# Routing logits of a linear-attention layer: from tokens on the output partitions to gate weights held in the array

## The reference

```
x = x + _layernorm(_L1_attn_ref(_layernorm(x), ...))          # linear attention, here "the linear layer"
xf = _layernorm(x).reshape(n, 256)                            # n = 8192 tokens
probs = softmax(xf @ Wg)                                      # Wg is 256 x 8: the routing logits
topv, topi = top_k(probs, 2)
... every token's row is sent to its two experts, positions by a running count ...
```

## Time and profile before

| | |
|---|---|
| median of 3 runs | 4360.51 us (4354.82 to 4367.13) |
| profiled execution | span 4370.4 us (no time other than the span is given for this execution) |
| PE busy | 91% of the span |
| DVE, ACT, POOL busy | 63%, 49%, 27% |
| mean granted TensorE clock | 0.957 of full speed |
| logits matmuls (L1585) | 256 records, first at 1622.4 us, last at 3465.3 us |

### The profile page before, as it was taken

How to read it: one execution, slowest core, us unless ns; L and a number is a source line. 1 busy time by engine, 2 the same in 40 slices (tenths; PEclk the granted TensorE clock), 3 DMA queues, 4 the chain that set the end, 5 groups by cost and what they waited for, 6 DMA issues and landing times. The chain is left out here.

```text
span 4370.4 us, 72366 instructions
## 1 busy us (share of the span) xinstructions
PE 3998.7 (91%) x27380; PEld 3076.0 (70%) x27380; DVE 2755.4 (63%) x8052; ACT 2120.4 (49%) x4002; POOL 1188.2 (27%) x1104
## 2 busy tenths in 40 slices
PE   5999999999995699999999999999999599999992
PEld 2344444444443588888888888888888599999992
DVE  4788888788781655556565555556665465555555
ACT  1566666666663445445454544445454133333333
POOL 3233343343422411111111111111111123333334
PEclk8899999999996899999999999999999799999996
DMA  4443443353230200000000000000000133333336
GB/s 76 87 94 64 84 103 61 73 115 70 42 80 24 78 11 25 21 20 25 24 21 18 18 16 21 11 19 19 19 19 31 34 74 70 63 63 73 63 66 184
DMA packets 176459, 226.91 MB, mean 52 GB/s; under 512 B 27292, under 2 KB 152571, under 8 KB 176112
## 3 DMA queue, kind: packets, MB, share of 16 engines
q1 hardware_dynamic: 148080, 185.86, 18.1%
q0 software_dynamic: 26736, 31.70, 4.7%
q10 hardware_dynamic: 1296, 4.72, 0.3%
HBM read 90.63 MB, written 87.05 MB: 41 GB/s over the span
## 5 line engine op out<-in xcount | busy, mean ns | idle before, releaser
L838 ACT ACTIVATE probs<-a_scores 128x1024 f32<-128x1024 f32 (+3 forms) x768 | 615.5, 812 | 334.6 <-PE a_scores L742 328.6
L996 DVE CUSTOM_DVE_ANT_0 a_scores<-a_scores,mask 128x384 f32<-128x384 f32 (+3 forms) x1024 | 480.5, 514 | 115.5 <-PE a_scores L728 109.8
L742 PEld LDWEIGHTS a_scores<-q_st,k_st 50*128 50x128 f32 x1536 | 147.9, 189 | 381.1 <-issue 245.0
L1732 ACT ACTIVATE l_o<-l_num,l_den 128x64 f32<-128x64 f32 x960 | 223.6, 317 | 352.2 <-DVE l_den L2124 349.6
L275 POOL TENSOR_TENSOR l_ln_rstd<-l_ln_ve,minus_half 128x4 f32<-128x4 f32 x80 | 84.1, 1051 | 1116.0 <-DVE l_ln_ve L248 1115.7
L999 DVE TENSOR_REDUCE mx<-a_scores 128x2 f32<-128x1024 f32 x256 | 310.5, 1223 | 83.1 <-PE a_scores L728 81.8
L742 PE MATMUL a_scores<-q_st,k_st 50*128 50x512 f32 (+3 forms) x1536 | 346.7, 449 | 9.2 <-DVE mx L996 4.4
L728 PE MATMUL a_scores<-k_st,q_st 48*128 48x512 f32 (+3 forms) x1536 | 304.7, 395 | 47.7 <-ACT probs L838 28.5
L762 PE MATMUL a_out<-probs,v_aug 128*32 128x512 f32 (+3 forms) x3072 | 344.8, 522 | 2.2 <-POOL probs L929 2.1
L929 POOL TENSOR_SCALAR_AFFINE_SELECT probs<-probs 128x512 f32<-128x512 f32 x256 | 163.6, 639 | 524.8 <-ACT probs L838 516.3
L2421 PE MATMUL e_out<-e_weights_hi,e_hT_hi 128*128 128x256 f32 x1088 | 303.9, 279 | 0.0
(11 more groups left out here) (268 smaller groups left out, 10506.6 us busy)
## 6 DMA issues: line engine op xcount, KB each, us to landing
q_st<-parts SPq DMA_DIRECT2D x192, 128.0 KB, 4.5
k_st<-parts SPq DMA_DIRECT2D x192, 128.0 KB, 6.2
expert_rows_scratch<-empty_row SPq DMA_DIRECT2D x34, 520.0 KB, 9.2
l_x<-x_scratch SPq DMA_DIRECT2D x32, 512.0 KB, 3.9
e_weights<-in_L_ffn_W_dram SPq DMA_DIRECT2D x16, 1024.0 KB, 6.8
e_rows<-expert_rows_scratch SPq DMA_DIRECT2D x24, 390.0 KB
e_rows<-expert_rows_scratch SPq DMA_DIRECT2D x16, 520.0 KB
x_in<-in_L_attn_x_dram SPq DMA_DIRECT2D x8, 1024.0 KB, 5.7
```

The costliest lines, as they stand in the source:

```text
L742: last = nc.tensor.matmul(psum_r[:, R.slot(u), h2, 0:w], k_st[rows, 2 * hg + pair, i * P:(i + 1) * P], q_st[rows, 2 * hg + pair, q0:q0 + w ...
L838: nc.scalar.activation(probs[:, k % 3, 2 * pair:2 * pair + 2, 0:w], psum_r[:, R.slot(u), :, 0:w], ACT.Exp).then_inc(R.evacuated[R.slot(u)], 1)
L996: last = nc.vector.tensor_tensor_reduce(s, s, mask[:, HALF - w:HALF], 1.0, LEAST, ALU.add, ALU.max, out[:, h2, :])
L1732: last = nc.scalar.activation(o[:, j % 2, head:head + DH1], psum_n[:, NUM.slot(n), h * DV:h * DV + DH1], ACT.Copy, scale=den[:, n % 2, 1, ...
```

## The change

The gate weights become the stationary operand and the tokens stream through. `wg` is padded from 8 to 32 columns (`EW = 32`, the rest filled with zeros by DVE ahead of the load), and the four token tiles of a group go to four groups of 32 columns of the array: tile j is written to partitions 32j to 32j+31 of one PSUM slot. That gives the logits with experts on the partitions and tokens on the free axis, as one unit `LT` in place of two units `L`. DVE copies the 128 x 128 block to SBUF (`lgT`, which lies in the bytes of `scores[:, 1]`, and so of `nT2`), PE turns it back by one transpose (unit `L`, `turn_logits`), and DVE copies the wanted 128 x (4 x 8) of it into `lg`. The number of units in the ring stays the same.

The place moves too: `LT` stands ahead of the last two `KT` units (now called `KE`), the transpose `L` behind them, and the wait for the last three `KT` units stays behind the transpose. `last_logits` waits for each `T3` unit by itself, just ahead of the half that reads it; in the tail this replaces the wait for both.

```diff
-    OWN = [("QK", NQK), ("KT", 8), ("O", 8), ("W", 2), ("T2", CD), ("F1", MF), ("F2", 2)]
+    OWN = [("QK", NQK), ("KT", 6), ("KE", 2), ("O", 8), ("W", 2), ("T2", CD), ("F1", MF), ("F2", 2)]
-    OF_LAST = [("T3", CD), ("L", 2)]
+    OF_LAST = [("T3", CD), ("LT", 1), ("L", 1)]
...
-        wg = sb("l_wg", [P, CD, E])
+        wg = sb("l_wg", [P, CD, EW])
...
+        lgT = scores[:, 1, 0, 0, :]
...
+                nc.vector.memset(wg[:, :, :], 0.0).then_inc(filled, 1)
...
-                    for i in range(2):
-                        u = U["L"] + i
-                        G.wait_free(pe, r, u)
-                        for jj in range(2):
-                            j = 2 * i + jj
-                            for c in range(CD):
-                                last = nc.tensor.matmul(psum_g[:, G.slot(u), jj * E:(jj + 1) * E],
-                                                        nT2[:, c, j * P:(j + 1) * P], wg[:, c, :],
-                                                        start=(c == 0), stop=(c == CD - 1))
-                        last.then_inc(G.full[G.slot(u)], 1)
+                    u = U["LT"]
+                    G.wait_free(pe, r, u)
+                    for c in range(CD):
+                        G.wait_evacuated(pe, r, U["T3"] + c)
+                        for j in range(G4):
+                            last = nc.tensor.matmul(psum_g[EW * j:EW * j + EW, G.slot(u), 0:P],
+                                                    wg[:, c, :], nT2[:, c, j * P:(j + 1) * P],
+                                                    start=(c == 0), stop=(c == CD - 1),
+                                                    skip_group_check=True)
+                    last.then_inc(G.full[G.slot(u)], 1)
+
+                def turn_logits(r, U):
+
+                    u = U["L"]
+                    G.wait_evacuated(pe, r, U["LT"])
+                    G.wait_free(pe, r, u)
+                    nc.tensor.transpose(psum_g[:, G.slot(u), 0:P], lgT[:, :], ident[:, :]
+                                        ).then_inc(G.full[G.slot(u)], 1)
...
+                    for i in range(8):
+                        u, j, half = kt_unit(U, i), i // 2, i % 2
+                        if i == 6 and not first:
+                            last_logits(g, U)
...
                     if not first:
-                        last_logits(g, U)
-
-                    for u in range(U["KT"] + 8 - R, U["KT"] + 8):
-                        G.wait_evacuated(pe, g, u)
+                        turn_logits(g, U)
+
+                    for i in range(8 - R, 8):
+                        G.wait_evacuated(pe, g, kt_unit(U, i))
...
                 turn_last(NGR - 1, NGR - 1, units_after)
-                for c in range(CD):
-                    G.wait_evacuated(pe, NGR - 1, units_after["T3"] + c)
                 last_logits(NGR - 1, units_after)
+                turn_logits(NGR - 1, units_after)
...
                 def keep_logits(r, g, U):
-                    for i in range(2):
-                        u = U["L"] + i
-                        G.wait_full(dve, r, u)
-                        nc.vector.tensor_copy(lg[:, 2 * i:2 * i + 2, :],
-                                              psum_g[:, G.slot(u), 0:2 * E].rearrange(
-                                                  "p (j e) -> p j e", j=2)).then_inc(G.evacuated[G.slot(u)], 1)
-                    G.wait_evacuated(dve, r, U["L"] + 1)
+                    u = U["LT"]
+                    G.wait_full(dve, r, u)
+                    nc.vector.tensor_copy(lgT[:, :], psum_g[:, G.slot(u), 0:P]
+                                          ).then_inc(G.evacuated[G.slot(u)], 1)
+                    u = U["L"]
+                    G.wait_full(dve, r, u)
+                    nc.vector.tensor_copy(lg[:, :, :],
+                                          psum_g[:, G.slot(u), 0:P].rearrange(
+                                              "p (j e) -> p j e", j=G4)[:, :, 0:E]
+                                          ).then_inc(G.evacuated[G.slot(u)], 1)
+                    G.wait_evacuated(dve, r, u)
```

More of the change, by code:

```diff
@@ L1169, in linear_layer @@
     NQK = 2 * NP
+    EW = 32
     LATE = 2
-    OWN = [("QK", NQK), ("KT", 8), ("O", 8), ("W", 2), ("T2", CD), ("F1", MF), ("F2", 2)]
+    OWN = [("QK", NQK), ("KT", 6), ("KE", 2), ("O", 8), ("W", 2), ("T2", CD), ("F1", MF), ("F2", 2)]
     OF_NEXT = [("T1", CD), ("V", 8 - LATE), ("VE", LATE)]
-    OF_LAST = [("T3", CD), ("L", 2)]
-    ORDER = OWN[0:1] + OF_LAST[0:1] + OWN[1:2] + OF_LAST[1:2] + OWN[2:3] + OF_NEXT[0:1] + OWN[3:4] + OF_NEXT[1:2] + OWN[4:5] + OF_NEXT[2:3] + OWN[5:]
+    OF_LAST = [("T3", CD), ("LT", 1), ("L", 1)]
+    ORDER = (OWN[0:1] + OF_LAST[0:1] + OWN[1:2] + OF_LAST[1:2] + OWN[2:3] + OF_LAST[2:3] + OWN[3:4] +
+             OF_NEXT[0:1] + OWN[4:5] + OF_NEXT[1:2] + OWN[5:6] + OF_NEXT[2:3] + OWN[6:])
     LAST_NORMS = (1, 2, 3, 5, 8, 9, 10, 12)
@@ L1329, in _ @@
                 nc.vector.tensor_copy(token[:, :], spot[:, :]).then_inc(filled, 1)
-                dve.wait_ge(filled, 2)
+                nc.vector.memset(wg[:, :, :], 0.0).then_inc(filled, 1)
+                dve.wait_ge(filled, 3)
         G = Ring(sem, "l_general", R, N_ALL)
@@ L1378, in v_unit, with kt_unit @@
             return U["V"] + i if i < 8 - LATE else U["VE"] + i - (8 - LATE)
+        def kt_unit(U, i):
+            return U["KT"] + i if i < 6 else U["KE"] + i - 6
         def of_group(view, g):
@@ L1408, in _ @@
                                          allow_slow_non_contiguous=True).then_inc(raw_loaded[0], 16)
-                for dst, w in ((raw_o[:, :, :], Wo), (raw_f[0], Wf1), (raw_f[1], Wf2), (wg[:, :, :], Wg)):
+                for dst, w in ((raw_o[:, :, :], Wo), (raw_f[0], Wf1), (raw_f[1], Wf2), (wg[:, :, 0:E], Wg)):
                     sp.dma_start(dst, w.rearrange("(c p) n -> p c n", p=P)).then_inc(load, 16)
@@ L1604, in group @@
                         G.wait_evacuated(pe, g, u)
[L1606 to L1614, removed]
+                    for i in range(8):
+                        u, j, half = kt_unit(U, i), i // 2, i % 2
+                        if i == 6 and not first:
+                            last_logits(g, U)
+                        G.wait_free(pe, g, u)
+                        for m in range(4):
+                            last = nc.tensor.transpose(psum_g[:, G.slot(u), m * P:(m + 1) * P],
+                                                       kT[:, 4 * half + m, j * P:(j + 1) * P],
+                                                       ident[:, :])
+                        last.then_inc(G.full[G.slot(u)], 1)
                     if not first:
-                        last_logits(g, U)
-                    for u in range(U["KT"] + 8 - R, U["KT"] + 8):
-                        G.wait_evacuated(pe, g, u)
+                        turn_logits(g, U)
+                    for i in range(8 - R, 8):
+                        G.wait_evacuated(pe, g, kt_unit(U, i))
                     if s == 0:
@@ L1758, in group @@
                     for i in range(8):
-                        u = U["KT"] + i
-                        j, half = i // 2, i % 2
+                        u, j, half = kt_unit(U, i), i // 2, i % 2
                         G.wait_full(act, g, u)
```

## The result

The changed kernel takes 4343.83 us (median of 20 runs, 4339.01 to 4363.79), the kernel before in the same comparison 4356.62 us (20 runs, 4348.15 to 4374.97). The ratio is 0.9977, with a 95% interval of 0.9966 to 0.9988: 0.23% or 10 us faster (5 to 15 us); the two medians by themselves are 12.8 us apart. Forecast were 7.7 us, and a change of less than 0.3% as the likely outcome; the measured gain agrees with both. Counted from its own starting point the range is 16.5 us faster to 5.5 us slower, and 10 us faster lies in it. As the experiments show, the 7.7 us were reached by a sum in which one term was too large and one was missing.

What follows compares the result with a forecast made beforehand. The prediction took PE's order to bound the kernel: 5.6 us from the groups plus 2.1 us from the tail, 7.7 us off the 4360.5 us median, gave 4352.8 us, with a range of 4344 to 4366 us.

Steps and rivals of the forecast that it cites:

- What bounds the kernel: Groups with logits: PE, busy 96%, sets the pace; an earlier `score(1)` moves all behind it.
- LT at 0.67 us: Each group: `LT`'s 16 records take PE 0.67 us, gaps included, where the old logits took 1.88; bounds 0.43 and 1.98.
- one after another: Rival, `LT`: column groups load weights serially, 1.98 us; 13.0 us slower in all, 4373.5 us; chance 0.08.
- the records stagger: Rival, `LT`: a matmul's second record waits for its first, 9 rounds, 1.2 us; no change, 4360.5 us; chance 0.10.
- no wait: Start of `LT`: its slot, `KT`'s unit 3, is copied out by 2240.20, before PE gets there at 2240.28.
- The trip to VectorE: Between `LT` and transpose `L`: DVE's copy, 0.29 us, is done 0.6 us ahead, covered by two `KE` units.
- The stall on ScalarE: Before `score(1)`: PE stands 0.7 us for ACT's last `kt` copy, leaving 0.37 us gain per group, 5.6 us in all.
- The tail: After the last group, once, at half clock: `choose` comes 2.1 us earlier; bounds 0.7 us lost and 2.5 us gained.
- At nothing: the wider `wg` and its memset.: Gate weights' load and setup: memset under 0.2 us if uncovered, DMA has the same rows; priced at nothing.
- The wait for ACT doesn't bind: Rival, before `score(1)`: ACT has `kt` out sooner, PE gains 1.09 us per group; 18.5 us, 4342 us; chance 0.04.
- The gain is taken back in the loop: Rival, chunk loop: something started ahead of the logits sets it, only the tail's gain stays; 4358 us; chance 0.12.

Runs made afterwards that it cites:

- the one-group run: Changed kernel with all four token tiles of `LT` in one group of 32 columns instead of four, only the first tile's logits as the reference's; one run, 4384.27 us.

## Why the prediction was right, and where it wasn't

*What bounds the kernel.* Right. PE's order sets the pace, and every experiment that moved `score(1)` moved the group by the same amount, to within 0.06 us.

*LT at 0.67 us.* Right, and for the reason given: four groups together. Counted as in the working, with the gap ahead, it is 0.67 us: the last transpose ahead of `LT` starts at 2228.90 and the next behind it at 2229.68, less the 0.11 us of one transpose. The 0.58 us above are without that gap. The array's part was taken as 0.43 us, and the 16 records start in four rounds of four, at 2229.10, 2229.23, 2229.34 and 2229.45. The rivals "one after another" (1.98) and "the records stagger" (1.2) are both out, and the one-group run shows what the first would have cost: 1.96 us, counted with the gap ahead. The Trainium skill's rule in "TensorE: Matmul & The Clock Gate", The mechanism, that a weight load overlaps matmuls in flight only in another row group, doesn't hold here: 16 loads of 110 ns in the same rows lie within 0.38 us, those of the second round from 2229.13 on, while the products that started at 2229.10 are in flight. The Trainium skill says in "TensorEngine Tiling (Array Packing)", Key Properties, that a change of tiling mode drains the array. The trace has 0.20 us from the last start of one form to the first of the next, on either side of `LT`, where one transpose follows another after 0.11. So it is some 0.09 us a side, where the working had 0.12 and 0.14; and the side ahead can't be told from a wait, as the trace has `LT`'s first load released by ACT's copy of its slot [0.17 <-ACT l_k L1776], where the working had "no wait".

*The trip to VectorE.* Right: 0.29 us copy, no wait.

*The stall on ScalarE.* Right as a mechanism, and ACT's last copy ended 5.21 us after `KT`'s start where the working has 5.23. The step that failed is the one from there to `score(1)`: "`score(1)` starts at 2242.71 to 2242.75", up to 0.05 us behind ACT's end. It is 0.21 us (2230.37 + 1.07 = 2231.44 to 2231.65), and 0.20 to 0.24 in every group. That made the term 5.6 us; it is 15 x 0.21 = 3.2 us. Why it takes that long isn't shown. It isn't the same at every wait: behind DVE's copy of `LT` the transpose follows 0.06 us later in all groups of the version with `LT` behind `KT`.

*The tail.* 2.1 us forecast, 6.49 - 4.45 = 2.04 measured.

*"At nothing: the wider `wg` and its memset."* Wrong. This is the term that was missing. I priced the memset and the DMA and not that the tiles behind move. It is the larger part of the gain: 0.41 us per group in the run with the wider tile alone (123.43 - 123.02), 0.35 in the changed kernel (0.56 less the 0.21 of the edited stretch), some 6 us over the groups.

The sum by the traces is 3.2 + 2.0 + 6 = 11 us, against 10 (5 to 15) measured. That the forecast's 7.7 lies inside the interval is luck in part: a 2.4 us overestimate and a 6 us omission partly cancelled. Without the side effect the change as such is worth 5 us by the traces, which this kernel's measurement can't tell from none.

*The other rivals.* "The wait for ACT doesn't bind" is out (0.77 us of idle time in each of 15 groups). "The gain is taken back in the loop" is out: `score(1)` to output projection is 45.32 us in both.

## What to carry to other kernels

Before pricing work taken off the busiest engine, look for the wait that this work covers; here half of the 1.88 us, 0.92, was cover for ScalarE's copies, and the cheapest remedy was to issue the next product that doesn't need them ahead of the wait. A cover moved to one trip uncovers another, so compare the lengths of both, hand-over included (from a copy's end to PE's next product it was 0.21 us behind ScalarE here and 0.06 behind VectorE). And when a tile changes its size, cut both traces at the same instructions and compare stretches that nobody edited: an allocation is an edit of everything behind it.

## What the runs showed of the hardware that I had not expected

The pace of PE products with 256 moving columns depended on where the operands' tiles lie: 11.43 to 11.68 us for the same 96 products. A shift of 256 bytes per partition gave the old pace back; one of 320 gave that of 64 in one stretch and only in part in the other. Which tile's place counts (the shifted stationary `hT`, against the unshifted weights, or a tile that another engine writes meanwhile) was not tried and stays open, and so does the reason why 64 + 256 bytes gave less than 64.

In most of these traces the spread between executions lies ahead of the linear part. Its first scores start at 1494.4 us in the profile before, at 1488.3 in the one after, and at 1475.3 and 1505.7 us in those of the 256-byte and the 128-byte shift, with the same instructions up to there but for one small memset in the changed kernel. The mean granted clock up to the first scores is 0.92, 0.93, 0.94 and 0.91 in these four, in the same order, so the later start goes with the lower clock. From then on groups without a fall of the clock repeat to 0.1 us in the kernel before and to 0.3 us in the changed one. Where the clock falls within the groups, as in the trace with the logits only moved, the spread lies there as well (16 us). A few us in the groups are seen in the trace long before they can be seen in the times.
